# Heads of an mLSTM: decays taken in place and in advance, values token-major, two batches' heads inside the feed-forward

## The reference

```python
logfg = log_sigmoid(f_pre); Fcum = cumsum(logfg)
Dmat = Fcum[..., :, None] - Fcum[..., None, :] + i_pre[..., None, :]   # causal, else -inf
m = max(Dmat); Smat = exp(Dmat - m)
qk = einsum('bhsd,bhtd->bhst', q, k) / sqrt(16)       # 8 heads, 16 wide
C = qk * Smat
n = maximum(abs(sum(C)), exp(-m))
h = einsum('bhst,bhtd->bhsd', C / n, v)               # v: 32 wide
h_out = sigmoid(o_pre) * (h * rsqrt(mean(h*h) + EPS) * mh_w)
x1 = x + h_out @ w_out
mlp = silu(h2 @ w_gate) * (h2 @ w_up) @ w_down        # h2 = rmsnorm(x1)
```

## Time and profile before

| | |
|---|---|
| Time, median of 3 runs | 752.77 us (749.85 to 752.94) |
| The profiled execution's own time | 753.29 us |
| Its span, first to last instruction | 751.5 us |
| TensorE busy | 712.5 us (95%), mean granted clock 0.935 |
| TensorE weight loads | 670.3 us (89%) |
| VectorE, ScalarE, GpSimd busy | 443.5, 423.5, 252.0 us |
| DMA | 69.63 MB |

### The profile page before, as it was taken

The page is one execution under the profiler, slowest core; times in us unless marked ns, Lnnn a source line. Parts: engine busy times, 40 slices in busy tenths (PEclk is TensorE's granted clock), DMA queues, the critical chain, the costliest instruction groups (busy, mean ns, idle before and its releaser), DMA issues. The chain is left out here.

```text
span 751.5 us, 15356 instructions
## 1 busy us (share of the span) xinstructions
PE 712.5 (95%) x5290; PEld 670.3 (89%) x5290; DVE 443.5 (59%) x961; ACT 423.5 (56%) x1106; POOL 252.0 (34%) x265
## 2 busy tenths in 40 slices
PE   8999999999999999999987999988998799999995
PEld 8999999999999999999877999987666579999995
DVE  6465665576655766566565655643155437655686
ACT  5566686667756677666684333366454544333553
POOL 3624742244422434224741411217254122111011
PEclk9999999999999999999999999998556659999998
DMA  6266644456343663436500400007320100000000
GB/s 228 72 209 196 174 131 123 119 167 176 118 119 100 181 181 102 131 96 185 169 3 4 159 2 0 15 11 235 113 69 15 44 0 1 2 0 0 1 28 28
DMA packets 44889, 69.63 MB, mean 93 GB/s; under 512 B 3376, under 2 KB 30640, under 8 KB 44592
## 3 DMA queue, kind: packets, MB, share of 16 engines
q1 hardware_dynamic: 44416, 68.31, 30.4%
q10 hardware_dynamic: 432, 0.79, 0.3%
HBM read 52.18 MB, written 16.91 MB: 92 GB/s over the span
## 5 line engine op out<-in xcount | busy, mean ns | idle before, releaser
L303 PE MATMUL PJ<-xTh,WBh 128*128 128x256 f32 x364 | 106.6, 293 | 0.4 <-POOL WBl L808 0.4
L305 PE MATMUL PJ<-xTh,WBl 128*128 128x256 f32 x364 | 102.7, 282 | 0.0
L304 PE MATMUL PJ<-xTl,WBh 128*128 128x256 f32 x364 | 102.7, 282 | 0.0
L545 ACT ACTIVATE probs<-SC,nmax 128x256 f32<-128x256 f32 x128 | 59.5, 471 | 63.9 <-DVE nmax L671 62.4
L793 POOL TENSOR_TENSOR stage<-stage 128x256 f32<-128x256 f32 x32 | 24.5, 765 | 164.1 <-DVE stage L659 164.1
L669 DVE TENSOR_REDUCE rmax<-SC 128x2 f32<-128x512 f32 x64 | 44.2, 691 | 54.4 <-PE SC L384 47.5
L1154 PE MATMUL UG<-xTh,WBh 128*128 (+1 forms) x256 | 73.5, 287 | 1.1 <-PEq L49 1.1
L552 ACT ACTIVATE probs<-probs,rinv 128x256 f32<-128x256 f32 x128 | 58.5, 509 | 27.2 <-DVE rinv L675 27.1
L1157 PE MATMUL UG<-xTh,WBl 128*128 (+1 forms) x256 | 72.4, 283 | 0.0
L1155 PE MATMUL UG<-xTl,WBh 128*128 (+1 forms) x256 | 72.4, 283 | 0.0
L303 PEld LDWEIGHTS PJ<-xTh,WBh 128*128 128x128 f32 x364 | 69.2, 190 | 1.0 <-issue 0.6
(11 more groups left out here) (252 smaller groups left out, 2453.4 us busy)
## 6 DMA issues: line engine op xcount, KB each, us to landing
K<-scr_k SPq DMA_DIRECT2D x60, 256.0 KB, 4.5
raw<-in_w_att SPq DMA_DIRECT2D x37, 256.0 KB, 4.7
Q<-scr_q SPq DMA_DIRECT2D x15, 512.0 KB, 7.4
stage<-scr_m SPq DMA_DIRECT2D x4, 1024.0 KB, 5.9
scr_q<-rot_h SPq DMA_DIRECT2D x30, 128.0 KB
scr_q<-rot_l SPq DMA_DIRECT2D x30, 128.0 KB
scr_k<-rot_h SPq DMA_DIRECT2D x30, 128.0 KB
scr_k<-rot_l SPq DMA_DIRECT2D x30, 128.0 KB
```

The source lines that it names most:

```text
L303: pe.matmul(out, ah, bh, start=(i == 0), stop=False)
L304: pe.matmul(out, ah, bl, start=False, stop=False)
L305: last = pe.matmul(out, al, bh, start=False, stop=(i == n - 1))
L545: last = act.activation(probs[:, j % 2, t, :], SC[j % 2][:, t, :], ACT.Exp, scale=SCALE, bias=nmax[:, j % 2, t:t + 1], accum_out=rsum[:, j ...
```

## The change

- **Decays in place.** `decay` writes exp over its own argument in `A`, no longer into `ga`. So it needs no free buffer and ScalarE can be any number of heads ahead. There are three buffers for four batches (a new `A2`; batch 3 takes `stage` again when batch 0's heads are weighed). All decays stand before the feed-forward on ScalarE. The copies `mlp_hi` of the weight pieces stand in other places among them.
- **Values token-major.** `values` has the weights as stationary operand (128 columns) and the values with their column of ones as moving one (33 columns). The result goes into the same bank as the scores, `SC` (banks 3 and 4 of five `UG`). `take_pair` and `back` are gone; `take(c, h)` copies two blocks of 33 columns per head, on VectorE for batches 0 and 1 and on ScalarE for 2 and 3. `scores` of a head waits for the `take` of the head two before.
- **Heads of batches 2 and 3 inside the feed-forward.** Its batch 0 has the heads of batch 2 in its eight steps, its batch 1 those of batch 3. It is written out for all four batches and has three banks in place of four. The end of batch c+1's heads stands in the steps of batch c.
- **Tanh output gate.** sigmoid(o) is taken as (1 + tanh(o/2))/2: ScalarE takes tanh, VectorE multiplies by 1 + t, and the factor 1/2 is in the head norm (`4.0 / DH`, `4.0 * RMS_EPS`).
- The column of ones is broadcast, `nm` is written over `cumS`, transposes and `project_out` share the bank `TB`, `hT` has a buffer of its own, and the int8 pieces are split in two groups of six.

```diff
-        A = [a[:, :].rearrange("p (h n) -> p h n", h=HM) for a in (stage, stage1)]
+        A = [a[:, :].rearrange("p (h n) -> p h n", h=HM) for a in (stage, stage1, A2, stage)]
...
-        UG = [pb(f"UG{i}") for i in range(4)]
+        UG = [pb(f"UG{i}") for i in range(5)]
+        SC = UG[3:5]
         OUTS = pb("OUTS", (P, 2, 512))
         TB = pb("TB")
-        X = pb("X")
...
             def m_rows(c):
-                if c > 1:
-                    sp.wait_ge(s_["e_ready"], HM * (c - 1))
-                src = scr_m[c:c + 1, 0:HM, :]
-                sp.dma_start(A[c % 2][:, :, 0:S], src.broadcast_to([P, HM, S])).then_inc(a_in[c % 2], 16)
-                sp.dma_start(A[c % 2][:, :, S:S + P], src[:, :, P:S].broadcast_to([P, HM, P])).then_inc(a_in[c % 2], 16)
+                if c == 2:
+                    sp.wait_ge(s_["vog_ready"], TT * B)
+                if c == 3:
+                    sp.wait_ge(s_["c_ready"], HM)
+                for i in range(2):
+                    src = scr_m[c:c + 1, 4 * i:4 * i + 4, :]
+                    sp.dma_start(half(c, i)[:, :, 0:S], src.broadcast_to([P, 4, S])).then_inc(a_in[c][i], 16)
+                    sp.dma_start(half(c, i)[:, :, S:S + P],
+                                 src[:, :, P:S].broadcast_to([P, 4, P])).then_inc(a_in[c][i], 16)
...
             more(RING, 10)
             m_rows(2)
+            m_rows(3)
             more(10, 12)
-            m_rows(3)
...
             def scores(c, h):
                 r, n = slice(32 * (h % 4), 32 * (h % 4) + 32), (h // 4) * S
-                if h == 0:
-                    pe.wait_ge(s_["qk_split"], 2 * B if c == 0 else 2 * (c + 1))
+                if h == 0 and c == 0:
+                    pe.wait_ge(s_["qk_split"], 2 * B)
+                    pe.wait_ge(s_["og_ready"], TT * B)
                 if c or h >= 2:
-                    pe.wait_ge(s_["c_ready"], HM * c + h - 1)
-                bank = UG[h % 2]
+                    pe.wait_ge(s_["taken"], HM * c + h - 1)
+                bank = SC[h % 2]
                 for keys, q, out in ((n, slice(n, n + S), bank[:, 0:S]), (n + P, slice(n + P, n + S), bank[:, S:S + P])):
                     pe.matmul(out, stack(c, 1)[r, keys:keys + P], stack(c, 0)[r, q], start=True, stop=False)
...
             def values(c, h):
                 pe.wait_ge(s_["c_ready"], HM * c + h + 1)
-                if c or h >= 4:
-                    pe.wait_ge(s_["vt_ready"], HM // 2 * c + h // 2 - 1)
-                w = gb[:, h % 2, :]
-                out = UG[2 + h // 2 % 2][0:DH + 1, h % 2 * S:(h % 2 + 1) * S]
-                pe.matmul(out[:, 0:P], V1[:, c, 0, h, :], w[:, 0:P], start=True, stop=True)
-                pe.matmul(out[:, P:S], V1[:, c, 0, h, :], w[:, P:S], start=True, stop=False)
-                pe.matmul(out[:, P:S], V1[:, c, 1, h, :], w[:, S:S + P], start=False,
-                          stop=True).then_inc(s_["pv_ready"], 1)
+                w, at = gw[:, h % 2, :], S + P
+                out = [SC[h % 2][:, at + t * VW:at + (t + 1) * VW] for t in range(TT)]
+                pe.matmul(out[0], w[:, 0:P], V1[:, c, 0, h, :], start=True, stop=True)
+                pe.matmul(out[1], w[:, P:S], V1[:, c, 0, h, :], start=True, stop=False)
+                pe.matmul(out[1], w[:, S:S + P], V1[:, c, 1, h, :], start=False, stop=True).then_inc(s_["pv_ready"], 1)
...
+            scores(0, 0)
+            for c in range(2):
+                for h in range(HM):
+                    if h < HM - 1:
+                        scores(c, h + 1)
+                    elif c == 0:
+                        scores(1, 0)
+                    values(c, h)
+                    if c and h == 2:
+                        heads_T(0)
+                    if c and h == 5:
+                        project_out(0)
+            pe_T(pe, 2, 0)
+            up, down = ffn_pe_parts(pe, 1)
             for c in range(B):
-                heads(c)
-            def finish_heads(k, c, ht):
-                if ht == 0:
-                    back(3, 3)
-                if ht == 2:
-                    pe_T(pe, 2, 2)
-                if ht == 4:
-                    heads_T(3)
-                if ht == 5:
-                    project_out(3)
-                if ht == 7:
-                    pe_T(pe, 2, 3)
-            ffn_pe(pe, 1, finish_heads)
+                for ht in range(FT):
+                    up(c, ht, c == 0)
+                    if c < 2:
+                        scores(c + 2, ht)
+                    if ht > LAG:
+                        down(c, ht - LAG, c == 0)
+                    elif ht < LAG and c:
+                        down(c - 1, ht + FT - LAG, c == 1)
+                    if c < 2 and ht:
+                        values(c + 2, ht - 1)
+                    elif c in (1, 2) and ht == 0:
+                        values(c + 1, HM - 1)
+                    if c < 3 and ht == 2:
+                        heads_T(c + 1)
+                    if c < 3 and ht == 3:
+                        project_out(c + 1)
+                    if c < 3 and ht == 5:
+                        pe_T(pe, 2, c + 1)
+                    if c in (1, 2) and ht == 7 or c == 3 and ht == 5:
+                        pe_T(pe, 3, c - 1)
+            for ht in range(FT - LAG, FT):
+                down(B - 1, ht, False)
             ffn_pe(pe, 2)
...
-                    act.activation(og_v[:, c, t, :], UG[2 + t][:, D:2 * D], ACT.Sigmoid).then_inc(s_["og_ready"], 1)
+                    act.activation(og_v[:, c, t, :], UG[2 + t][:, D:2 * D], ACT.Tanh, scale=0.5).then_inc(s_["og_ready"], 1)
...
             def decay(c, h):
                 if h % 4 == 0:
                     act.wait_ge(s_["masked"], 2 * c + h // 4 + 1)
-                if c or h >= 2:
-                    act.wait_ge(s_["c_ready"], HM * c + h - 1)
-                e, a, at = ga[:, h % 2, :], A[c % 2], 32 * c + h
-                act.activation(e[:, 0:S], a[:, h, 0:S], ACT.Exp, scale=-1.0, bias=gcol[:, 0, at:at + 1])
-                act.activation(e[:, S:S + P], a[:, h, S:S + P], ACT.Exp, scale=-1.0,
+                e, at = A[c][:, h, :], 32 * c + h
+                act.activation(e[:, 0:S], e[:, 0:S], ACT.Exp, scale=-1.0, bias=gcol[:, 0, at:at + 1])
+                act.activation(e[:, S:S + P], e[:, S:S + P], ACT.Exp, scale=-1.0,
                                bias=gcol[:, 1, at:at + 1]).then_inc(s_["e_ready"], 1)
...
+            def take(c, h):
+                act.wait_ge(s_["pv_ready"], HM * c + h + 1)
+                if h == 0 and c >= 2:
+                    act.wait_ge(s_["hs_ready"], c - 1)
+                act.activation(hraw_v(c)[:, :, h, :],
+                               SC[h % 2][:, S + P:S + P + TT * VW].rearrange("p (t n) -> p t n", t=TT),
+                               ACT.Copy).then_inc(s_["taken"], 1)
...
-            mlp_hi(0, 2)
+            mlp_hi(0, 5)
             gates()
             evac(1)
-            mlp_hi(2, 4)
             evac(2)
-            mlp_hi(4, 5)
+            mlp_hi(5, 7)
             evac(3)
             exp_nm()
+            for h in range(HM):
+                decay(0, h)
+            mlp_hi(7, 10)
+            for h in range(HM):
+                decay(1, h)
+            squares(0)
+            for h in range(HM):
+                decay(2, h)
+                if h == 3:
+                    hoT(0)
+                if h == 6:
+                    act_ssq(act, 2, 0)
+            mlp_hi(10, 12)
+            act_hi(act, 2, 0)
+            for h in range(HM):
+                decay(3, h)
+            silu, hi = ffn_act_parts(act, 1)
...
+                for ht in range(FT):
+                    silu(c, ht, c == 0)
+                    if ht:
+                        hi(c, ht - 1)
+                    elif c:
+                        hi(c - 1, FT - 1)
+                    if c < 2 and ht:
+                        take(c + 2, ht - 1)
+                    elif c in (1, 2) and ht == 0:
+                        take(c + 1, HM - 1)
+                    if c < 3:
+                        if ht == 0:
+                            squares(c + 1)
+                        if ht == 3:
+                            hoT(c + 1)
+                        if ht == 5:
+                            act_ssq(act, 2, c + 1)
+                        if ht == 6:
+                            act_hi(act, 2, c + 1)
+                    if c >= 2 and ht == 0:
+                        act_hi(act, 3, c - 2)
+                    if c == 3 and ht == 6:
+                        act_hi(act, 3, 2)
+            hi(B - 1, FT - 1)
             ffn_act(act, 2)
         @block.vector
...
+                    if c < 2:
+                        weigh(c + 2, ht)
+                    if c < 3:
+                        if ht == 0:
+                            norm_a(c + 1)
+                        if ht == 1:
+                            norm_b(c + 1)
+                        if ht == 3:
+                            hoT(c + 1)
+                        if ht == 4:
```

(36 more changed lines are left out.)

348 lines of the change are left out of this document (153 added, 195 removed).

## The result

| | before | changed |
|---|---|---|
| Time, median of 4 runs | 751.8 us (749.85 to 752.94) | 773.95 us (771.35 to 777.77) |
| Ratio | | 1.0296, 95% interval 1.0270 to 1.0322 |
| Profiled execution, its time and span | 753.29, 751.5 us | 774.23, 772.6 us |
| TensorE busy, mean clock | 712.5 us, 0.935 | 711.1 us, 0.931 |
| VectorE, ScalarE, GpSimd busy | 443.5, 423.5, 252.0 us | 439.4, 409.0, 251.3 us |

A forecast was written before the change was run, and what follows sets the result against it. The prediction took TensorE to bound heads (mostly at 1.2 GHz) and feed-forward. First feed-forward matmul at 572.6, plus 118.5, clock 4 and last feed-forward 56.7 made a 751.8 span; with 1.8 around it, 753.6 us, range 742 to 765.

The forecast's parts named there:

- Step 1: Start of the heads: ScalarE waits for two weight pieces before batch 3's evacuation, so the first weighing comes 5.4 us later.
- rival E: Start of the heads: the early pieces land earlier and don't hold ScalarE, 5.4 less, 748 us; chance 0.06.
- Step 2: Batches 0 and 1 alone: 2.45 us a head, slow normalization beside the masks, first feed-forward matmul at 572.6.
- Step 3: Feed-forward with heads inside: 93.5 us of TensorE work and 25.0 of waits, 118.5 in all, plus 4 for the clock.
- (c): Feed-forward, heads_T to project_out: TensorE waits 2.35, 2.7 and 2.5 us with only one short step between.
- (d): Feed-forward, squares to the transposes of step 5: TensorE waits 3.25, 3.25 and 2.75 us.
- (b): Feed-forward, norm of the heads: TensorE waits 3.15, 0.55 and 2.35 us for batches 1, 2 and 3.
- (a): Start of the feed-forward: TensorE waits 2.15 us, as batch 3's decays and the Silu table precede the first silu.
- (e): Clock in the feed-forward: one in three of eight waits brings a drop of about 1.9 us, +4, bounds 0 and 15.
- C: Feed-forward's first three batches: clock falls at nearly every wait, 15 us instead of 4, 761 us; chance 0.20.
- D: Value passes: stationary load bounds them, 1.42 us as before, 7 more in heads alone, 2.5 in feed-forward, 763; chance 0.12.
- B: Heads and feed-forward: value passes are cheap and the clock holds, 745 us; chance 0.28.

The follow-up runs named there:

- e1: Changed kernel, but ScalarE takes weight pieces 5 and 6 after batch 0's decays, not ahead of batch 3's evacuation: 764.1 us, ratio 1.014 to the kernel before.
- v1: Changed kernel with 64 instead of 33 moving columns in every value matmul: 772.68 us, ratio 1.0277 to the kernel before.
- e4: Changed kernel, but values of batches 0 and 1 go to other banks than the scores: 771.19 us, ratio 1.0233 to the kernel before.
- m1: Changed kernel, but GpSimd adds batch 3's masks only after VectorE has normalized batch 0: 770.52 us, ratio 1.026 to the kernel before.
- a1: f1 plus unread matmuls before and behind the transposition ahead of the feed-forward, 16 and 8: 766.7 us, ratio 1.0191 to the kernel before.
- f1: Changed kernel with 14 unread matmuls ahead of each heads_T, project_out and transposition in the feed-forward's first three batches: 767.74 us, ratio 1.021 to the kernel before.
- a2: a1 with e2's edit: 762.39 us, ratio 1.0138 to the kernel before.
- e2: Changed kernel, but batch 3's decays and weight pieces 10 and 11 stand ahead of batch 0's squares: 780.8 us, ratio 1.0404 to the kernel before.
- c2: Changed kernel with e1's and e4's edits and the hooks inside the feed-forward a step later: 744.63 us, ratio 0.9894 to the kernel before.
- d1: e4 plus four unread matmuls after each head's values in batches 0 and 1: 777.57 us, ratio 1.0358 to the kernel before.
- c1: Changed kernel with e1's edit and the hooks inside the feed-forward a step later: 744.77 us, ratio 0.991 to the kernel before.
- t1: c2 plus 16 unread matmuls ahead of the last transposition before the feed-forward and 8 behind it: 738.9 us, ratio 0.984 to the kernel before.

## Why the prediction was wrong

- **Step 1, the start: right in kind, a little small.** ScalarE idles until the pieces land; rival E, that it would not, falls. 5.4 was forecast; 7.0 came (520.04 to 527.02), as the piece landed later than the earlier trace rows said, and e1 brings all of it back.
- **Step 2, a head at 2.45 us: the step that failed first.** The term "values taken 0.9, near the middle" was 1.29 (six passes of 0.215). v1 shows that the 33 moving columns do not set it, so the end of 0.35 could not hold; the bound 1.57 from the transposes and the old 1.42 were the nearer rows, and the forecast averaged between two mechanisms of which one had to hold. The copy's wait was about right (0.5 forecast with its hops; 0.39 by e4). Eleven heads lie on the way to the feed-forward (eight to the head scales of batch 0, three after heads_T) and make 4.4 of the 7.9 us. The others ran while ho was made, and only shortened TensorE's wait for it, to 2.3 us; the forecast has 3.6, or 4.0 if its own 25.7 is added to 525.5.
- **Step 2, the normalization beside the masks: right.** 4.15 and 0.69 us, and 3.4 won back in m1. Not in the forecast were the same contention on the scaling of x (1.63 for 0.62, 1.0 us), the sum of batch 0 standing on VectorE behind the copy of a head, which waits for its values (1.0 us, at 574.50), and project_out at the low clock (2.8 us for 2.0). With the heads that is 7.2 of the 7.9.
- **Step 3, waits: right place, smaller.** (c) and (d) came about as forecast, (b) for one batch of three: 17.5 in sum against 25.0. Term (a), 2.15 for the decays and the table, did not show: TensorE at the low clock was slower than they. a1 made it appear (2.72).
- **Step 3, a head inside the feed-forward at 0.9 us: mis-sized.** "Half of step 2's" carried the 0.9 of the values over and halved it, and counted nothing for the change from one kind of matmul to the other. A head cost 1.44 at the high clock, 16 of them some 8.6 us more than forecast.
- **Step 3 (e), the clock at +4: the step that failed worst.** It cost 16.3 us by the window of the stage. "One in three" was counted from three places; here the clock fell at five of seven waits, where the +4 has two falls of 1.9. A fall cost what was forecast: 10.0 us for the five together. And the forecast had only a first step at the low clock, where the stage was entered at 0.50 and stayed there for 12.5 us (6.3). That the clock answers to the rests is shown by f1, 6.2 us faster with 126 matmuls more, and by a2, where at 1.00 throughout the stage is 10.6 us shorter, filling included. (a2 has e2's edit too, which alone left the first batch as it was.)
- **The rivals.** C (clock, 15 instead of 4) and D (passes no cheaper than before) both came true. Each was priced alone, at 761 and 763, and given 0.20 and 0.12 as if the other then could not hold. With C at its 15, together they make 753.6 + 11 + 9.4 = 774.0, and 773.95 was measured. That they agree so well is luck: the waits were 7.5 shorter, the heads inside the feed-forward 8.6 dearer where D had 2.5, those ahead of it 4.4 where D had 7, and the start 1.5 longer. But the range left out a sum that its own prices gave. B is refuted on both counts.
- **The end at 56.7 us and TensorE's total: right.** The last feed-forward was untouched.

## What to carry over

Price a short matmul by its stationary columns as well as by its moving ones, and take the larger, never the mean: here 33 stationary by 128 moving columns and 128 by 33 took the same 0.215 us a pass. When work is hung into another loop, place each piece a full step behind what it needs: here one step later was worth 21 us in that stage, since most rests cost their own length and then the clock. And rivals that rest on different mechanisms can hold together: add them for the end of the range.

## What was not expected of the hardware

- A pass with 128 stationary and 33 moving columns took 0.215 us at a granted clock of 0.50 and 0.11 to 0.12 at 1.00: its price goes with the clock.
- TensorE kept the low clock through 30 us without a gap in c2 (0.50 at 15.66 of 15.70 and 15.00 of 15.00 us busy), and in d1 at 50.9 of 52 us. So being busy did not by itself bring the clock back. In c1 the same instructions were at 1.00 after 12 us; what decides between the two is open.
- Adding matmuls whose output nothing reads made the kernel faster: 126 of them by 6.2 us (f1), 24 of them by 5.7 in the median, with all five runs at one time where c2 had two (t1).
- VectorE is held up beside GpSimd where both read and write wide tiles of SBUF: 4.87 us for 1.47 (m1), 1.63 for 0.62. GpSimd hardly was (4.83 us for the masks, 4.66 in m1). And the weighings, which read the scores out of PSUM, took 0.56 us beside the masks of batch 2 (535.9 to 540.6) as they did elsewhere.
